# One more tile per batch through the dense table product, 27 tiles gathered instead of 28, and one dense pass of each slot at another place

## The reference, cut to what matters

```python
q = (x @ Wq).reshape(b, n, HEADS, DIM) * DIM ** (-0.5)
sim = jnp.einsum('pbnhd,pkhd->pbnhk', q_pk, pk_keys)      # 2 sides, 128 keys each
scores, idx = jax.lax.top_k(sim, 16)
index = idx[0][..., :, None] + 128 * idx[1][..., None, :] # 256 pairs, a row of the table each
final_scores, pk_idx = jax.lax.top_k(score, 16)           # the best 16 pairs
kv_scores = jax.nn.softmax(final_scores)
k = jnp.einsum('bnhk,bnhkd->bnhd', kv_scores, keys_table[ind])
v = jnp.einsum('bnhk,bnhkd->bnhd', kv_scores, values_table[ind])
out = causal_attention(q, k, v) ; return out @ Wo
```

## Time and profile before

| | |
|---|---|
| median of three runs | 9090.88 us |
| the profiled execution | 9084.84 us, span 9083.0 us |
| PE busy, weight loads busy | 87%, 68% of the span |
| DVE, ACT, POOL busy | 78%, 54%, 75% |
| mean granted TensorE clock | 0.928 |
| dense table loads (SP queue) | 512 of 1024 KB |
| indirect gathers (POOL queue) | 7168 |

### The profile page before, as it was taken

The page is one execution under the profiler, slowest core; times in us unless marked ns, Lnnn a source line. Parts: engine busy times, 40 slices in busy tenths (PEclk is TensorE's granted clock), DMA queues, the critical chain, the costliest instruction groups (busy, mean ns, idle before and its releaser), DMA issues.

```text
span 9083.0 us, 179526 instructions
## 1 busy us (share of the span) xinstructions
PE 7878.3 (87%) x51232; PEld 6137.2 (68%) x51232; DVE 7108.3 (78%) x30205; ACT 4886.8 (54%) x14163; POOL 6820.4 (75%) x7177
## 2 busy tenths in 40 slices
PE   5988888888888888888888888898888888889898
PEld 4766667667666766766667666676766766667676
DVE  7787787777878778787787877878778787787875
ACT  3555555555555555555555555464555555555554
POOL 5777777777777777777777777777777777777777
PEclk7999999999999999999999999999999999999998
DMA  4555555555555555555555555555555555555554
GB/s 133 170 171 165 168 168 170 168 167 167 172 165 167 171 166 168 170 167 166 166 172 166 168 169 168 168 171 168 169 166 169 168 166 170 172 162 171 162 179 146
DMA packets 445970, 1516.75 MB, mean 167 GB/s; under 512 B 123760, under 2 KB 141552, under 8 KB 379248
## 3 DMA queue, kind: packets, MB, share of 16 engines
q0 software_dynamic: 344064, 939.98, 33.8%
q1 hardware_dynamic: 100848, 564.37, 17.1%
HBM read 1499.66 MB, written 4.19 MB: 166 GB/s over the span
## 4 chain that ended last, share of the span: by engine, by line
POOL 49%; issue 18%; PE 16%; DVE 15%; ACT 1%; DMA 1%; POOLq 0%; DVEq 0%; SPq 0%; ACTq 0%
POOL got L391 49%; PE dense_ps L523 6%; DVE wide L1214 4%; PE comb_ps L664 3%; DVE hits L1178 2%; DVE chosen L1109 2%; PE wideT_ps L509 2%; DVE onehot L1104 1%; PE front_ps L463 1%; DVE onehot L1097 1%; PE score_ps L499 1%; DMA got<-in_table,rows 1%; DVE lifted L1117 1%; PE score_ps L548 1%; PE front_ps L467 1%
## 5 line engine op out<-in xcount | busy, mean ns | idle before, releaser
L391 POOL DMA_INDIRECT got<-in_table,rows x7168 | 6818.5, 951 | 2245.6 <-issue 2168.4
L523 PE MATMUL dense_ps<-tab,wideT 128*128 128x256 f32 x16384 | 4030.5, 390 | 10.6 <-ACT kv_d L725 9.4
L523 PEld LDWEIGHTS dense_ps<-tab,wideT 128*128 128x128 f32 x16384 | 3053.3, 195 | 669.9 <-issue 265.1
L1214 DVE SCALAR_TENSOR_TENSOR wide<-const_ps,rank,expo 128x128 f32<-128x128 f32 x8192 | 2299.3, 343 | 1357.6 <-PE wideT_ps L509 1039.4
L790 ACT ACTIVATE expo<-sim_d,shift 128x128 f32<-128x128 f32 x8192 | 2598.9, 394 | 128.8 <-DVE wide L1214 127.9
L725 ACT ACTIVATE wideT<-wideT_ps 128x512 f32<-128x512 f32 x2048 | 1212.9, 592 | 676.6 <-PE wideT_ps L509 669.9
L509 PE MATMUL wideT_ps<-ident,wide 128*128 128x128 f32 x8192 | 1255.4, 276 | 265.7 <-ACT wideT L725 243.1
L509 PEld LDWEIGHTS wideT_ps<-ident,wide 128*128 128x128 f32 x8192 | 1023.3, 143 | 534.4 <-issue 286.3
L664 PE MATMUL comb_ps<-got,spread 128*32 128x256 f32 x14336 | 1031.5, 436 | 135.6 <-DMA got<-in_table,rows 107.8
L664 PEld LDWEIGHTS comb_ps<-got,spread 128*32 128x32 f32 x14336 | 469.6, 122 | 587.7 <-issue 245.1
L725 ACT ACTIVATE kv<-comb_ps,wsum 128x256 f32<-128x256 f32 x448 | 210.4, 470 | 909.3 <-PE comb_ps L664 909.1
(11 more groups left out here) (167 smaller groups left out, 7386.0 us busy)
## 6 DMA issues: line engine op xcount, KB each, us to landing
tab<-in_dense SPq DMA_DIRECT2D x512, 1024.0 KB
got<-in_table,rows POOLq DMA_INDIRECT x7168, 2.7
adj_i<-in_adj SPq DMA_DIRECT2D x16, 1024.0 KB
x_in<-in_x SPq DMA_DIRECT2D x16, 256.0 KB, 6.4
out<-fin SPq DMA_DIRECT2D x16, 256.0 KB, 6.0
tab<-in_wqpk_t SPq DMA_DIRECT2D x1, 512.0 KB, 10.5
tab<-in_keys_t SPq DMA_DIRECT2D x1, 512.0 KB, 14.8
wq_sb<-in_wq SPq DMA_DIRECT2D x1, 512.0 KB, 13.5
```

The source lines that it names most:

```text
L391: pool.indirect_dma_start(out=got[got_no(n)][:, g, :], out_offset=None, in_=table, in_offset=bass.IndirectOffsetOnAxis(ap=rows[:, t * GATH ...
L523: mm = pe.matmul(dense_ps[:, v * 2 * D:(v + 1) * 2 * D], wideT[k % 2][:, (2 * u + v) * P:(2 * u + v + 1) * P], tab[(k // CHUNK) % 2][:, (2 ...
L1214: last = dve.scalar_tensor_tensor(wide[k % 2][:, 2 * u + v, :], count_ps[:, v, :], rank1[:, 2 * half + v, key:key + 1], expo[k % 2][:, 2 * ...
```

## The change

The last tile of head 4 (slot EXTRA_SLOT = 19) is no longer gathered. It becomes a third part of the dense work: "half" 2, one tile with its own table, 128 keys in 32 passes of four keys each. A batch has 160 passes in the order half 0 (64), half 2 (32), half 1 (64). Its result goes to `kv[:, 3]` by `take_extra`, and slot 19 runs the attention as before. POOL skips the slot, so that the three `got` buffers rotate over 27 tiles. The chunk size stays 8 keys, so a batch loads 48 chunks, and in half 2 a chunk serves two passes. The third part brings its own similarities (`front_dense`), ranking (`rank_dense` of one tile), two sets of hits and sums; the pair in head 4 that held the tile shrinks to one tile.

Half 1 is prepared later than before (slots 6 to 14 in place of 0 to 8), half 2 in slots 0 to 4; hits lie in slots 4, 12, 14, 24 and 26.

The plans hold 160 passes: MIDDLE puts 88 in the even and 72 in the odd slots (an EIGHT is new). The place w[1] moves: from before `scores` to between `values` and `project` on PE, after `take_headT` on ACT, and behind the passes of w[4] on DVE, ahead of `sum_rows`, `lift` and `add`.

```diff
+EXTRA = 4
+EXTRA_SLOT = EXTRA * T + T - 1
+GSLOTS = SLOTS - 1
...
+EXTRA_PASSES = NKEYS // 4
+PASSES = 2 * HALF_PASSES + EXTRA_PASSES
+PART = {0: 0, 2: HALF_PASSES, 1: HALF_PASSES + EXTRA_PASSES}
...
+EIGHT = (2, 1, 2, 2, 1)
 NONE = (0, 0, 0, 0, 0)
 MIDDLE = [
-    FIVE, FOUR, FOUR, THREE,
-    SIX, FOUR, FIVE, THREE,
-    SIX, FIVE, FIVE, FOUR,
-    SIX, FIVE, FIVE, THREE,
-    SIX, FOUR, FIVE, FOUR,
-    SIX, FOUR, FIVE, THREE,
-    SIX, FIVE, FOUR, THREE]
+    EIGHT, SIX, FIVE, FOUR,
+    SIX, SEVEN, SIX, THREE,
+    SEVEN, SEVEN, SEVEN, FOUR,
+    SIX, SIX, FOUR, FIVE,
+    EIGHT, SIX, SIX, FIVE,
+    EIGHT, FIVE, SEVEN, FOUR,
+    SIX, SEVEN, FOUR, THREE]
...
-HITS = {1: {4: (0, 1), 8: (2, 3)}, 0: {24: (0, 1), 26: (2, 3)}}
+HITS = {2: {4: (0, 1)}, 1: {12: (0, 1), 14: (2, 3)}, 0: {24: (0, 1), 26: (2, 3)}}
...
+def places(k):
+
+    half, r = part_of(k)
+    if half == 2:
+        return [(j, 4 * r + j, 0) for j in range(4)]
+    return [(2 * u + v, 2 * r + u, v) for u in range(2) for v in range(2)]
...
             if not (first and c < 2):
-                sp.wait_ge(dense_done, b * PASSES + (c - 1) * CHUNK)
-            k = (c % (CHUNKS // 2)) * KEYS
+                sp.wait_ge(dense_done, b * PASSES + (chunk_end(c - 2) if c >= 2 else chunk_end(c - 2 + CHUNKS) - PASSES))
...
-                h, t = n // T, n % T
-                slot = b * SLOTS + n
+                t = n % T
+                if n == EXTRA_SLOT:
+                    continue
+                slot = gslot(b, n)
...
                 if not (first and n < 3):
-                    pool.wait_ge(combined, slot - (got_back(n) - 1))
+                    pool.wait_ge(combined, slot - 2)
...
                     key_transpose_dense(c, tile, fronts(b, n, last))
-                k = passes(b, k, w[1], first)
                 if t == 0:
                     pe.wait_ge(q_copied, s + 1)
...
                 values(slot, t)
                 if tile is not None:
                     values_dense(c, tile)
+                k = passes(b, k, w[1], first)
                 project(slot, h)
...
+        def take_extra(b, n):
+
+            assert EXTRA_SLOT - T < n < EXTRA_SLOT
+            act.wait_ge(dense_done, b * PASSES + PART[1])
+            act.wait_ge(z_ready, b * 3 + (ORDER[2] + 1))
+            copy(kv[:, T - 1, :], dense_ps[:, 0:2 * D], scale=z_inv[:, T:T + 1]).then_inc(kv_x_copied, 1)
...
                 if half is not None and o == 2:
                     best_dense(half, 0)
-                k = passes(b, k, w[1], last)
                 hit_part(1)
...
                 k = passes(b, k, w[4], last)
+                k = passes(b, k, w[1], last)
                 if more and t % 2 == 1:
                     sum_rows(nt)
```

More of the change, by code:

```diff
@@ L81, with pair, tiles, tiles_before @@
 PAIRS = [(0, 2), (2, 2)]
+def pair(h, i):
+    return (2, 1) if h == EXTRA and i == 1 else PAIRS[i]
+def tiles(h):
+    return T - 1 if h == EXTRA else T
+def tiles_before(b, h):
+    if h == GH:
+        return (b + 1) * GSLOTS
+    return b * GSLOTS + (h * T - (1 if h > EXTRA else 0))
+def gslot(b, n):
+    return b * GSLOTS + (n - (1 if n > EXTRA_SLOT else 0))
+def part_of(k):
+    half = 0 if k < PART[2] else 2 if k < PART[1] else 1
+    return half, k - PART[half]
+def places(k):
[3 more added lines that the diff above has]
+    return [(2 * u + v, 2 * r + u, v) for u in range(2) for v in range(2)]
+def chunk_of(k):
+    half, r = part_of(k)
+    return ORDER[half] * PART_CHUNKS + r // (2 if half == 2 else 4)
+def chunk_end(c):
+    return next(k + 1 for k in reversed(range(PASSES)) if chunk_of(k) == c)
+def prep(b, n, last):
+    if n < 6:
+        return 2, b, n
+    if n < 15:
+        return 1, b, n - 6
+    if n >= 20 and not last:
+        return 0, b + 1, n - 20
+    return None, b, -1
+def sets_before(n, last):
+    return 4 + sum(len(g) for half in (2, 1, 0) if not (half == 0 and last)
+                   for m, g in HITS[half].items() if m < n)
 FIRST_TILES = [(0, 1), (1, 1), (2, 2)]
@@ L98, in got_no @@
 def got_no(n):
-    return n % 3 if n < SLOTS - 1 else 1
-def got_back(n):
-    return next(d for d in range(1, 6) if got_no((n - d) % SLOTS) == got_no(n))
+    return (n - (1 if n > EXTRA_SLOT else 0)) % 3
 def dense_tile(b, n, first, last):
@@ L355, in batch @@
             for c in range(CHUNKS):
-                if c == 5 and not first:
+                if c == 6 and not first:
                     store(b - 1)
@@ L931, in batch @@
                     exponent_dense(c, tile)
-                k = passes(b, k, w[3], first, last)
+                k = passes(b, k, w[3], first, last, n)
                 take_probT(slot, t)
@@ L935, in batch @@
                     take_probT_dense(c, tile)
-                k = passes(b, k, w[4], first, last)
+                k = passes(b, k, w[4], first, last, n)
                 take_headT(slot)
@@ L939, in batch @@
                     take_headT_dense(c)
+                k = passes(b, k, w[1], first, last, n)
         schedule(act, first, batch)
@@ L1295, in first @@
             best_dense(0, 1)
-            count_dense()
+            count_dense(0)
             norm_dense(0, 0)
@@ L1312, in batch @@
                 more = not (last and h == GH - 1)
-                m = (s + 1) * T
-                t0, nt = PAIRS[t // 2]
-                half, of_d, o = None, b, n - PREP[1]
-                if n <= max(HITS[1]):
-                    half = 1
-                elif n >= PREP[0] and not last:
-                    half, of_d, o = 0, b + 1, n - PREP[0]
-                sets = HITS[1].get(n, ()) if half == 1 else HITS[0].get(n, ()) if half == 0 else ()
+                m = tiles_before(b, h + 1)
+                t0, nt = pair((h + 1) % GH, t // 2)
+                half, of_d, o = prep(b, n, last)
+                sets = () if half is None else HITS[half].get(n, ())
                 def hit_part(part):
```

281 lines of the change are left out of this document (150 added, 131 removed).

## The result

The changed kernel takes 10043.76 us (four runs, 10035.57 to 10054.49) against 9091.05 us before: a ratio of 1.105, interval 1.103 to 1.107. The forecast was 9675 us with a range from 9300 to 10000, so the direction was right and the size was not: the change costs 953 us where 584 were forecast. The profiled execution took 10038.7 us, its span is 10036.9.

What follows compares the result with a forecast made beforehand. POOL's gathers bound the kernel before, PE's chain afterwards: 526.9 us work + 51.1 idle + 24.6 clock = 602.6 us a batch, taken as 599 between this and 594.9; with the end batches 9675 us, 6.4% slower, range 9300 to 10000.

Steps and rivals of the forecast that it cites:

- POOL is the bound before, with little slack behind it: Gathers on POOL pace the loop at 561.7 of 562.7 us a batch; PE's waits for gathered rows, 7.6 us, are all the slack.
- A pass costs PE 2.16 us, and the bound moves to PE's chain: Dense passes on PE: 32 more add 69.1 us a batch; PE's work becomes 526.9 us, 97% of POOL's new floor of 541.6.
- The rival by which POOL stays the bound: PE has room for 32 passes, only gathers are late: 8770 us, faster; weight loads busy 68% speak for it; chance 0.06.
- The small parts: On PE, per batch: hits +2.1 us, one more `front_dense` product +0.6, dropped tile's products -2.0, its share of `move` -0.3.
- The clock: PE's loss to the lower clock tied to its idle time: 51.1 x 0.48 = 24.6 us a batch.
- The moved pass: w[1] moved: `keyT` waits +5.0 us, `headT` waits -6.2, DVE's changes cancel; -1.2 us of PE idle a batch.
- The rival by which it hurts: In 21 slots `keyT` waits for a group of exponentials on ACT: 39 us a batch with the clock, 10300 us; chance 0.05.
- The filling of idle time: 18 of 32 passes in odd slots each fill up to 1.04 us of PE's wait for `lifted`: some 15.5 us a batch.
- The wait for `wideT`: PE's wait in slots with hits: 15.9 us a batch before, +4.5 net as hits leave slot 8 for slots 12 and 14.
- The second way to the sum: Factor 1.129 from slots 4 to 19 of the last batch, applied to PE's 526.9 us of work: 594.9 us a batch.
- The own range of the main case: Idle time of 36 to 66 us a batch with its clock loss: 580 to 625 us a batch, 9370 to 10080 us.
- The table: Chunks serving two passes in the third part: 0 taken; rival that all 16 come late: 31 us a batch, 10180 us, chance 0.05.

## Why the prediction was right or wrong

*POOL is the bound before, with little slack behind it: right.* Two kernels bear it out: with POOL relieved the time fell by 26 us of 321, and with PE's waits for `wideT` shortened alone it did not fall at all. The 7.6 us were a little too many: 1.8 of them are waits for DVE, not POOL (`comb_ps <- DVEq` in the earlier trace rows), and 1.3 of these are still there with 27 tiles.

*A pass costs PE 2.16 us, and the bound moves to PE's chain: right.* In the rows of slot 4 and around it the transposes of two passes in a row start at 5189.16 and 5191.33. PE's work came out at 527 us a batch. The rival by which POOL stays the bound is out, and with it the reading of the weight loads' 68% as room for 32 more passes. My reason was too strong, though: I wrote that the products, not the loads, fill the 2.16 us. In a window over two passes in a row (length, busy us of PE, PEld, DVE, ACT, POOL) the loads fill most of it too:

```profile
5187.33:5191.65 4.32, 4.32 (x27) 3.81 (x24) 1.78 (x7) 2.33 (x8) 3.10 (x5) 1.00 0.34 104
```

The Trainium skill ("Perfetto Trace Analysis", "Identifying the Most-Contended Engine") has TensorE's headroom judged by weight-load busy time, beside the share of the peak FLOP rate. This trace agrees in part: where passes stand back to back the loads are busy 3.81 of 4.32 us, 88%, so with these fp32 products they read an eighth low when PE has no gap. Part of the rest of the way down to 68% is PE's idle time, 13% of a batch, which the new passes hardly filled.

*The small parts: right in sum. The clock: right by luck.* 0.34 us of clock loss per us of idle was measured where 0.48 was taken, but on more idle time: 24.7 against 24.6. Over all the kernels here the ratio lies between 0.25 and 0.49, so tying the loss to the idle time was no sound step.

*The moved pass: right in `headT` and nearly in `keyT`, wrong in the rest.* I had -1.2 us of idle a batch and took what happens on DVE to cancel out. It doesn't: against the kernel with the pass put back, `wideT` rises by 6.1 us a batch and `lifted` falls by 2.8, with `keyT` at +6.8 and `headT` at -6.2; the idle time is 2.4 us longer. Undone, the move still costs 66 us, 4 a batch, since the clock gives back more. The rival by which it hurts is out.

*The filling of idle time: the step that failed.* I took 18 passes in odd slots to fill 15.5 us of the wait for `lifted`; the wait fell by 2.6, from 23.3 to 20.7 us a batch. The kernels between the two split this. It is 26.9 us with 27 tiles and none of the new passes, 23.5 with the 32 passes and the pass put back, and 20.7 with the moved pass. So the passes filled 3.4 us, not 15.5. The step "it fills up to 1.04 us of waiting for DVE" went wrong in three ways.

First, I took DVE to be the late engine through the whole slot. In slots 5, 9, 13 and 25, which got 8 of the 18 passes, the wait went from 7.7 us to 4.0 together, and these 4.0 are tails: DVE's `sum_rows` and `lift` behind its last pass. With one more pass in each of them (the kernel with the fuller odd slots) slots 5, 13 and 25 still wait 0.97 us each.

Second, I counted the preparation of the dense parts by its amount ("the tile's ranking only changes its name") and not by its place. DVE's total is as forecast (487 us a batch, 489 forecast), but in the changed kernel half 1 is ranked in slot 7. Its `move` in batch 8, before and after:

```profile
4747.67 1.06 PE L499 MATMUL score_ps<-group_of,lifted 128*128 128x16 f32 x8 [0.91 <-DVE lifted L1117]
```

```profile
5266.74 1.89 PE L577 MATMUL score_ps<-group_of,lifted 128*128 128x16 f32 x8 [3.12 <-DVE lifted L1207]
```

With 27 tiles and the dense ranking in slot 11, slot 7 waits 0.9 us and slot 11 2.9; in the changed kernel slot 11 waits 1.2. The three odd slots in which dense tiles are ranked (1, 7 and 21) hold 7.8 of the 20.7 us, and the plan gave them 2, 0 and 1 passes more.

Third, a pass fills only where DVE has something else to do at that moment. The change from FOUR to SIX put its second pass in w[0], where DVE was already waiting for PE, and DVE waits longer for PE's transposes than before (65.5 us a batch before, 917.2 / 14; 78.5 after, 1098.3 / 14). For `lifted` this is a small part: one pass in w[0] takes it down by 1.0 us only. The prediction had read the earlier trace rows by slots, as busy shares, and not asked at which point of a slot DVE's idle time lies.

*The wait for `wideT`, 27.3 us where I took 20.4.* With the pass put back it is 21.3, so 6.1 of the 6.9 us too many come with the moved pass. The rest is near, but not by my reasoning: I let 4.3 us go with the hits of slot 8, and slot 8 still waits 3.5 us without any hits, because of the second pass in its w[0].

*The second way to the sum, the factor 1.129 of the densest stretch: wrong.* Measured it is 623.8 / 527 = 1.18. The stretch, slots 4 to 19, leaves out slots 20 to 27, where DVE ranks and makes the hits for the next batch's half 0; I had named the graph layer and passed over that. It is not the whole of it, for slots 4 to 19 of batch 8 alone have a factor of 354.37 / 305 = 1.16 in the changed kernel. Averaging the two ways moved the forecast 3.6 us a batch further off. The own range of the main case, to 10080 us, would have held the result, though with an idle time of up to 66 us a batch and not 72.

*The table: 1.6 us a batch, small as taken.* A cost of 0 was too low, and the rival's 31 far off.

*What stays open.* The moved pass was told apart only as a whole: why the clock is granted at its upper level longer with it (0.953 against 0.944 in the mean of the execution) though PE's idle time is about the same, the runs don't show. Slot 7, where half 1's ranking now falls together with a plan of three passes, was not changed by itself; that the ranking makes its wait is read from the kernel that has it in slot 11. Why the moved pass lets `wideT` wait longer was not followed through a slot, nor were the waits of slots 14 and 26, which stay with one pass in w[0].

## What to carry to other kernels

When the engine that paces a kernel is relieved, first ask by how much the next chain is behind it: as long as that chain stays as it is, the waits of the others for that engine are the most there is to gain (here under 7.6 us a batch, of 20, and some 2 came). When work is added to a second engine, its price is the spacing in the timeline and not the sum of busy times, and it fills another engine's lateness only if it is put between pieces of that engine's work; at a point where that engine already waits, it delays what is queued behind. Nor can it shorten a tail of that engine's own work at the end of a stage. So look at where in a stage the idle time of the partner lies, with two rows of the timeline, before counting on it.

## What the runs showed of the hardware

The clock loss does not follow the idle time alone: with the pass put back PE was idle 69.6 us a batch and lost 31.3 us to the lower level, in the changed kernel 72.0 and 24.7, and with passes moved to odd slots 62.3 and 16.3. Which lengths of stall cost the clock was not tried by itself.
